# Feed-forward of a two-layer transformer block: the down-projection between the gate half and the value half

## The chip, the cores and the metric

The kernel runs on 1 core of one Trainium2 chip. The time is device time in microseconds, the median of the runs shown. A NeuronCore's engines are named here as in the profile: PE (TensorE, matmuls; PEld is its weight load), DVE (VectorE), ACT (ScalarE), POOL (GpSimd), SP (SyncE, which issues nearly all DMA). They run their own queues in order and wait for one another by semaphores.

## The reference

The inputs are x and ctx of shape 4 x 1024 x 512 in float32. First a banded attention (each query sees the keys within 128 rows), then two layers of local attention and feed-forward. What the change touches is the feed-forward of `_layer`, with HID = 1365:

```python
h = shift_token(x)
mu = h.mean(-1, keepdims=True)
var = h.var(-1, keepdims=True)
h = (h - mu) / jnp.sqrt(var + 1e-05) * lg + lb
h = h @ w1 + b1                       # w1: 512 x 2730
a, g = jnp.split(h, 2, axis=-1)       # value, gate
h = a * jax.nn.gelu(g, approximate=False)
x = x + h @ w2 + b2                   # w2: 1365 x 512
```

## The kernel before

The 4096 rows are 32 tiles of 128 rows (`TILES`). The kernel has a band stage and then, for each of two layers, `attend(l)` and `ffn(l)`. A float32 product is made of three matmuls: every operand is split into a high part, rounded to the type `fp32r`, and the low rest, and TensorE adds high x high, low x high and high x low in PSUM (`products`, L728 to L731, and the loop of `up`, L1069 to L1073).

The feed-forward works on groups of 4 tiles (`GROUP`), so 8 groups (`GROUPS`) of 512 rows in each layer. The 1365 hidden columns are 11 blocks (`HC`): ten of 128 and one of 85 (`FULL`, j = 10). For one group g and one block j:

- `up(l, g, j, 0)` is the gate half: 12 matmuls (4 chunks of the 512 input columns, three each) of 512 rows into one PSUM bank. `up(l, g, j, 1)` is the value half, 12 more into another bank. Three banks go round among the halves (`up_bank`, L365), so the gate half of a block waits until `u` of the block two before it is made, and the value half until the gate of the block before it is read (L1068).
- ACT makes the gate, `gate` (L1401): GELU of the first bank plus bias. DVE makes `u` (`make_u`, L1775): value plus bias, times gate. ACT writes the high part of it into `uT` (`split_u`, L1412, its instruction at L1135), DVE the low part (`split_u`, L1784, its instruction at L1462). The ring of `uT` has three slots.
- `down(g, j)` (L1080) waits for the low part (`uT_low`) and adds the block's share of the output into four banks, one for each tile of the group: 4 x 3 matmuls. For j = 10 in groups 0 to 6 it is a stacked form with 8 matmuls (L1093 to L1099): two transfers on SP (`stack_u`, L681) copy the low part into the unused partitions of `uT`, and `down` waits for them (`u_stacked`), as does ACT's gate of block 1 of the next group (L1407).
- The first `down` of a group overwrites the four banks, so it waits for `f_out` tile by tile: DVE's `finish_group` (L1793, its instruction at L1799) adds the banks of the group before to the residual. It stands in DVE's queue behind `make_u` and `split_u` of block 1 (L1804 to L1811).

In the same period DVE, POOL and ACT prepare the next group's input: `moments`, POOL's `inverse_deviation`, `normalise` at blocks 1, 3, 5, 7; TensorE's transposes `turn_normalised` (L1047) at blocks 3, 5, 7, 9, with the copy on ACT and the low part on DVE (`split_normalised`). In group 0 of each layer the weights of the blocks are split as well: ACT rounds block j+2 behind its part of `uT` (L1434), DVE subtracts (L1809), and ACT writes the high part of block j+1 ahead of the gate of block j (L1428). In the last group of layer 0 ACT and DVE split the next layer's attention weights (L1438 to L1443, L1817).

The order on TensorE is written out by hand in `ffn` (L1105 to L1124). For one block it is gate half, value half, then the down-projection of the block before. At j = 1 that is `down(g - 1, FULL)`, at j = 2 both `down(g, 0)` and `down(g, 1)`, and in j = 0 there is none. Behind the last block of layer 0 come 24 matmuls of the next layer's projection (`project`, L804, L1123) and then `down(GROUPS - 1, FULL)`; behind the last block of layer 1 comes `down` alone. The first halves of a layer (group 0: block 0 and the gate half of block 1) are issued at the end of `attend`.

Of the kernel before, what the change touches and what calls it, by code (L numbers as in the profile page):

```python
# [51 lines left out]
def hid_rows(j):  # L52
    return min(P, HID - j * P)
# [123 lines left out]
def build(nc, x, ctx, mask, wqkv, q_scale, k_scale, wo, ln_g, ln_b, w1, b1, w2, b2, consts, out):  # L177
# [162 lines left out]
    def turned_u(l, g, j):  # L340
        return ffns[l].uT[(g * HC + j) % 3]

    def w1_part(block, j, half, c):
        n = hid_rows(j)
        at = (half * KC + c) * n
        return block[:, at:at + n]

    def w2_part(block, j):
        n = hid_rows(j)
        return block[0:n, 2 * KC * n:2 * KC * n + DIM]  # L350
# [10 lines left out]
    def stacked(g, j):  # L361

        return j == FULL and g < GROUPS - 1

    def up_bank(m):  # L365

        return bank_pair[:, m, :] if m < 2 else banks[2 + (m + 1) % 3]
# [352 lines left out]
    def tensor_program(e):  # L720
# [7 lines left out]
        def products(bank, lhs, rhs, first, last):  # L728
            e.matmul(bank, lhs[0], rhs[0], start=first, stop=False)  # L729
            e.matmul(bank, lhs[1], rhs[0], start=False, stop=False)  # L730
            return e.matmul(bank, lhs[0], rhs[1], start=False, stop=last)  # L731
# [63 lines left out]
        def turn_first_rows(l):  # L795
            n = l * TILES
            w.wait_ge(S("s_in", n % 2), lap(n, 2, 32))
            if l:
                w.wait_ge(S("fhT_low"), n)
            else:  # L800
                w.wait_ge(S("queryT_low"), TILES)
            transposes(rows_bank(l, 0), attends[l].h_in[n % 2], KC, S("h_turned"))

        def project(l, t, first, last):  # L804
            A, base = attends[l], l * TILES
            n = base + t
            for at in range(first, last):
                part, (c, i) = PARTS[at // 12], divmod(at % 12, 3)
                bank = banks[0] if part == 2 else qk_banks(t)[:, part, :]
                if (c, i) == (0, 0):  # L810
                    w.wait_ge(S("hT_low"), n + 1)
                    w.wait_ge(S("attend_weight_high"), KC * (4 * l + at // 12 + 1))
                    if part == 2:
                        w.wait_ge(S("v_rows"), n)
                        w.wait_ge(S("a_out"), base + max(0, t - 3))
                        if t == 0:
                            w.wait_ge(S("f_out") if l else S("keyT_low"), base - 3 if l else TILES)
                    elif t > 1:
                        w.wait_ge(S("with_sin"), 2 * n - 1 + part)
                    elif t:  # L820
                        w.wait_ge(S("f_out") if l else S("x1") if part else S("total_low"),
                                  base - 2 + part if l else TILES if part else BATCH)
                    elif l:
                        w.wait_ge(S("gate") if part else S("u"), l * GROUPS * HC - 1 + part)
                    else:
                        w.wait_ge(S("score_max"), TILES)
                cols = slice(part * DIM, (part + 1) * DIM)
                ins = e.matmul(bank, A.hT[n % 2][:, i % 2, c * P:(c + 1) * P], (wqkv_l if i == 2 else wqkv_h)[:, c, cols],  # L828
                               start=(c, i) == (0, 0), stop=(c, i) == (KC - 1, 2))
                if (c, i) == (KC - 1, 2) and part:  # L830
                    ins.then_inc(S("v_projected") if part == 2 else S("qk_projected"), 1)
# [215 lines left out]
        def turn_normalised(l, t):  # L1047
            n = l * TILES + t
            w.wait_ge(S("ln_normed"), n + 1)
            w.wait_ge(S("fhT_low"), n)  # L1050
            w.wait_ge(S("oT_low"), (l + 1) * TILES)
            transposes(banks[5], ffns[l].h_norm[n % 2], KC, S("fh_turned"))

        def wait_block(l, j):
            w.wait_ge(S("ffn_weight_high"), (HC + 1) * l + (j + 1 if j < FULL else HC + 1))

        def up(l, g, j, order, first=0, last=KC):

            Fm, base, step = ffns[l], l * TILES, l * GROUPS * HC
            n, half = hid_rows(j), 1 - order  # L1060
            hT, m = Fm.hT[g % 2], 2 * (g * HC + j) + order
            bank = up_bank(m)
            w.wait_ge(S("fhT_low"), base + GROUP * (g + 1))
            wait_block(l, j)
            if 2 <= m <= 4:
                w.wait_ge(S("lprobT"), PAIRS * (base + TILES))
            elif m > 4:
                w.wait_ge(S("u") if (m - 3) % 2 else S("gate"), step + (m - 3) // 2 + 1)  # L1068
            for c in range(first, last):  # L1069
                high, low = w1_part(Fm.block_h[j], j, half, c), w1_part(Fm.block_l[j], j, half, c)  # L1070
                e.matmul(bank[0:n, :], high, hT[:, 0, c, :], start=c == 0, stop=False)  # L1071
                e.matmul(bank[0:n, :], high, hT[:, 1, c, :], start=False, stop=False)  # L1072
                ins = e.matmul(bank[0:n, :], low, hT[:, 0, c, :], start=False, stop=c == KC - 1)  # L1073
            if last == KC:
                ins.then_inc(S("up_gate") if half else S("up"), 1)

        def ffn(l):
            Fm, base, step = ffns[l], l * TILES, l * GROUPS * HC

            def down(g, j):  # L1080
                n, q = hid_rows(j), step + g * HC + j
                uT = turned_u(l, g, j)
                w.wait_ge(S("uT_low"), q + 1)
                wait_block(l, j)
                for i in range(GROUP):
                    if j == 0:
                        if g:
                            w.wait_ge(S("f_out"), base + (g - 1) * GROUP + i + 1)
                        else:
                            w.wait_ge(S("a_out"), base + TILES)  # L1090
                            w.wait_ge(S("lprobT"), PAIRS * (base + TILES))
                    rows_of = slice(i * P, (i + 1) * P)
                    if stacked(g, j):  # L1093
                        at = 2 * KC * n
                        w.wait_ge(S("weights_stacked"), 32 * (l + 1))
                        w.wait_ge(S("u_stacked"), 32 * (l * (GROUPS - 1) + g + 1))
                        e.matmul(y_banks[i], uT[:, 0, rows_of], Fm.block_h[j][:, at:at + DIM], start=False, stop=False)
                        ins = e.matmul(y_banks[i], uT[0:2 * SHORT - SPARE, 1, rows_of],
                                       Fm.block_l[j][0:2 * SHORT - SPARE, at:at + DIM], start=False, stop=True)  # L1099
                    else:  # L1100
                        ins = products(y_banks[i], [uT[0:n, h, rows_of] for h in (0, 1)],
                                       (w2_part(Fm.block_h[j], j), w2_part(Fm.block_l[j], j)), j == 0, j == FULL)
                    ins.then_inc(S("down"), 1)

            up(l, 0, 1, 1)  # L1105
            for g in range(GROUPS):
                for j in range(HC):
                    if (g, j) < (0, 2):
                        continue
                    for order in (0, 1):  # L1110
                        up(l, g, j, order)
                    if j == 1:
                        down(g - 1, FULL)
                    if j == 2:
                        down(g, 0)
                    if j >= 2:
                        down(g, j - 1)
                    if g + 1 < GROUPS and j in (3, 5, 7, 9):
                        turn_normalised(l, (g + 1) * GROUP + (j - 3) // 2)
                    if l + 1 < DEPTH and (g, j) == (GROUPS - 1, 9):  # L1120
                        turn_first_rows(l + 1)
            if l + 1 < DEPTH:
                project(l + 1, 0, 12, 36)  # L1123
            down(GROUPS - 1, FULL)  # L1124

        band()
        for l in range(DEPTH):
            attend(l)
            ffn(l)
# [946 lines left out]
```

## Time and profile before

| what | us |
|---|---|
| median of 3 timed runs | 2969.84 (2969.80 to 2969.89) |
| span of the profiled execution (first to last instruction) | 2968.6 |
| PE busy | 2948.6 (99%) |
| DVE busy | 1621.6 (55%) |
| ACT busy | 1228.2 (41%) |
| POOL busy | 1151.9 (39%) |

Of the profiled execution the page gives the span; the time around it is the 1.2 us by which the timed runs exceed it. The busy time of PE is modelled at its ends, so 99% doesn't say that it computes at its peak: matmuls overlap one another. What tells the pace is the distance from one weight load to the next. The feed-forward of layer 0 takes the span from about 854 to 1589 us, that of layer 1 from about 2236 to its end.

### The profile page before, as it was taken

How to read it: one execution, taken by the hardware profiler on the slowest of the kernel's cores; microseconds unless marked ns; L12 is line 12 of the kernel's file. 1: busy time of each engine (PE TensorE's matmuls, PEld its weight loads, DVE VectorE, ACT ScalarE, POOL GpSimd, SP SyncE). 2: the span in 40 equal slices, each digit the busy share in tenths (PEclk: the TensorE clock that was granted, in tenths of full speed). 3: DMA queues.
4: the chain of work that ended last, by engine and by line, in shares of the span. 5: the costliest groups of instructions: out<-in, count | busy, mean ns of one | idle time of the engine just before them, and what ended most of it. 6: DMA issues, size and time to landing. Idle time of an engine off the chain costs nothing. (4 is left out here: it accounts for less than half of the span.)

```text
span 2968.6 us, 44295 instructions
## 1 busy us (share of the span) xinstructions
PE 2948.6 (99%) x17064; PEld 2417.8 (81%) x17064; DVE 1621.6 (55%) x3367; ACT 1228.2 (41%) x2501; POOL 1151.9 (39%) x1190
## 2 busy tenths in 40 slices
PE   9999999999999999999999999999999999999999
PEld 7887888888878888888887888888878888888887
DVE  8976767766664333333425767776775333333331
ACT  7875555555563111111124555555565211111111
POOL 7856666665621110111113556656651111221111
PEclk9999999999999999999999999999999999999999
DMA  6751111111151011100121111111133111111110
GB/s 220 235 186 45 34 51 54 44 44 54 33 158 39 20 40 45 46 31 21 40 96 60 44 43 44 58 47 33 54 93 100 58 45 46 40 59 56 48 49 25
DMA packets 143189, 188.43 MB, mean 63 GB/s; under 512 B 21366, under 2 KB 75130, under 8 KB 142980
## 3 DMA queue, kind: packets, MB, share of 16 engines
q1 hardware_dynamic: 142836, 185.54, 19.5%
q8 instruction: 135, 2.21, 0.3%
q14 instruction: 74, 0.61, 0.1%
q10 hardware_dynamic: 144, 0.07, 0.0%
HBM read 130.34 MB, written 52.46 MB: 62 GB/s over the span
## 5 line engine op out<-in xcount | busy, mean ns | idle before, releaser
L1071 PE MATMUL quad<-fhT_f,w_h_f 128*128 128x512 f32 (+1 forms) x1392 | 550.8, 396 | 0.0
L1073 PE MATMUL quad<-fhT_f,w_l_f 128*128 128x512 f32 (+1 forms) x1392 | 544.9, 391 | 0.0
L1072 PE MATMUL quad<-fhT_f,w_h_f 128*128 128x512 f32 (+1 forms) x1392 | 543.4, 390 | 0.0
L1780 DVE SCALAR_TENSOR_TENSOR u_f<-quad,bias_f,gate_f_raw 128x512 f32<-128x512 f32 (+1 forms) x174 | 130.4, 749 | 705.2 <-PE quad L1073 621.9
L1853 POOL TENSOR_SCALAR stats<-stats 128x1 f32<-128x1 f32 x64 | 43.4, 678 | 1017.1 <-DVE stats L1755 1016.4
L1303 ACT ACTIVATE lprob<-lprob,small 128x384 f32<-128x384 f32 (+2 forms) x512 | 288.6, 565 | 159.4 <-DVE small L1623 159.4
L1947 POOL TENSOR_TENSOR turned_qk<-with_cos,with_sin 128x256 f32<-128x256 f32 x252 | 181.0, 739 | 442.5 <-DVE with_sin L1647 386.4
L1409 ACT ACTIVATE gate_f_raw<-quad,bias_f 128x512 f32<-128x512 f32 (+1 forms) x174 | 119.5, 687 | 512.0 <-PE quad L1073 512.0
L1135 ACT ACTIVATE uT_f<-u_f 128x512 fp32r<-128x512 f32 (+2 forms) x176 | 117.3, 666 | 503.7 <-DVE u_f L1780 503.7
L828 PE MATMUL bank_pair<-wqkv_h,hT 128*128 128x512 f32 x992 | 318.9, 402 | 0.0
L1073 PEld LDWEIGHTS quad<-fhT_f,w_l_f 128*128 128x128 f32 (+1 forms) x1392 | 256.8, 184 | 63.1
L1072 PEld LDWEIGHTS quad<-fhT_f,w_h_f 128*128 128x128 f32 (+1 forms) x1392 | 257.1, 185 | 59.0
L1071 PEld LDWEIGHTS quad<-fhT_f,w_h_f 128*128 128x128 f32 (+1 forms) x1392 | 257.1, 185 | 58.2 <-issue 0.3
L1623 DVE CUSTOM_DVE_ANT_0 lprob<-quad,far 128x384 f32<-128x384 f32 (+2 forms) x512 | 228.7, 502 | 74.4 <-PE quad L920 74.4
L1938 POOL TENSOR_SCALAR lprob<-lprob,small 128x384 f32<-128x384 f32 (+2 forms) x192 | 226.4, 1186 | 26.4 <-DVE small L1608 26.4
L1135 ACT ACTIVATE lprobT<-quad 128x768 f32<-128x768 f32 (+2 forms) x256 | 173.0, 728 | 71.9 <-PE quad L942 69.3
L828 PEld LDWEIGHTS bank_pair<-wqkv_h,hT 128*128 128x128 f32 x992 | 177.4, 189 | 29.8
L828 PE MATMUL bank_pair<-wqkv_l,hT 128*128 128x512 f32 x496 | 200.9, 405 | 0.0
L1888 POOL TENSOR_TENSOR norm<-norm,half_power 128x16 f32<-128x16 f32 x64 | 196.1, 3063 | 5.3
L1462 DVE TENSOR_TENSOR uT_f<-u_f,uT_f 128x512 fp32r<-128x512 f32 x162 | 114.9, 709 | 111.8 <-ACT uT_f L1135 111.8
L959 PE MATMUL bank<-lprobT,v_rows 128*64 128x128 f32 x2688 | 175.0, 277 | 0.0
L959 PEld LDWEIGHTS bank<-lprobT,v_rows 128*64 128x64 f32 x2688 | 144.1, 137 | 34.4 <-issue 31.5
(236 smaller groups left out, 6047.9 us busy)
## 6 DMA issues: line engine op xcount, KB each, us to landing
s_in<-stream SPq DMA_DIRECT2D x128, 128.0 KB, 2.7
s_res<-stream SPq DMA_DIRECT2D x64, 256.0 KB, 2.9
stream<-a_out SPq DMA_DIRECT2D x64, 256.0 KB, 2.0
w_h_f_raw<-in_L_ffn_w SPq DMA_DIRECT2D x60, 256.0 KB, 5.2
h_in_f<-stream SPq DMA_DIRECT2D x112, 128.0 KB, 2.5
res_f<-stream SPq DMA_DIRECT2D x47, 256.0 KB, 3.1
x_in<-in_x SPq DMA_DIRECT2D x32, 256.0 KB, 3.0
x_dram<-x_out SPq DMA_DIRECT2D x32, 256.0 KB, 2.4
```

The costliest lines, as they stand in the source:

```text
L828: ins = e.matmul(bank, A.hT[n % 2][:, i % 2, c * P:(c + 1) * P], (wqkv_l if i == 2 else wqkv_h)[:, c, cols], start=(c, i) == (0, 0), stop= ...
L959: ins = e.matmul(banks[5][half, p * P:(p + 1) * P], A.v_rows[:, k - tiles + 1 + j, h * HD:(h + 1) * HD], A.probT[p % 2][:, i, j * P:(j + 1 ...
L1071: e.matmul(bank[0:n, :], high, hT[:, 0, c, :], start=c == 0, stop=False)
L1072: e.matmul(bank[0:n, :], high, hT[:, 1, c, :], start=False, stop=False)
L1073: ins = e.matmul(bank[0:n, :], low, hT[:, 0, c, :], start=False, stop=c == KC - 1)
L1135: return e.activation(to, source, ACT.Copy)
L1303: e.activation(prob, prob, ACT.Exp, bias=sm[:, h:h + 1], scale=-1.0, accum_out=sm[:, 8 + h:9 + h]).then_inc(S("lprob"), 1)
L1623: e.tensor_tensor_reduce(A.prob[h // 2][:, h % 2, 0:cols], quad[:, pair_banks(h // 2) + h % 2, 0:cols], A.far[:, WIN - cols:], 1.0, BIG, A ...
L1780: e.scalar_tensor_tensor(out=Fm.u[q % 2][0:n, :], in0=up_bank(2 * (g * HC + j) + 1)[0:n, :], scalar=Fm.bias1[0:n, 0, j:j + 1], in1=Fm.gate ...
L1888: e.tensor_tensor(nm[:, 16:32], nm[:, 0:16], half_power[:, :], ALU.pow).then_inc(S("norm_inverse"), 1)
L1938: e.tensor_scalar(prob, prob, sm[:, 16 + 2 * p:17 + 2 * p], None, ALU.mult).then_inc(S("pscaled_pool"), 1)
L1947: e.tensor_tensor(turned[:, :, a:a + h2], cos[:, :, a:a + h2], sin[:, :, b:b + h2], ALU.add).then_inc(S("rotated"), 1)
```

## The change

The down-projections move from behind the value half of a block to a place between its gate half and its value half. The transposes of the next group's input and everything behind them stay behind the value half. Nothing else is edited; the other engines' programs are the same.

```diff
@@ -1107,14 +1107,14 @@
                 for j in range(HC):
                     if (g, j) < (0, 2):
                         continue
-                    for order in (0, 1):
-                        up(l, g, j, order)
+                    up(l, g, j, 0)
                     if j == 1:
                         down(g - 1, FULL)
                     if j == 2:
                         down(g, 0)
                     if j >= 2:
                         down(g, j - 1)
+                    up(l, g, j, 1)
                     if g + 1 < GROUPS and j in (3, 5, 7, 9):
                         turn_normalised(l, (g + 1) * GROUP + (j - 3) // 2)
                     if l + 1 < DEPTH and (g, j) == (GROUPS - 1, 9):
```

## Rows read from the trace of the kernel before

**Rows 1.** The page, part 1: busy us, share of the span, instructions of each engine.
```profile
PE 2948.6 (99%) x17064; PEld 2417.8 (81%) x17064; DVE 1621.6 (55%) x3367; ACT 1228.2 (41%) x2501; POOL 1151.9 (39%) x1190
```

**Rows 2.** Waits of PE and PEld: who waited for whom, us in total, times, longest.
```profile
PE bank_pair L1071 <- DVE fhT_f L1462: 0.8, 2, 0.4
...
PEld quad L920 <- issue: 24.5, 128, 0.6
```

**Rows 3.** Timeline, group 2 of layer 0: start us, us, engine, line, operation, out<-in, [idle before].
```profile
1106.51 0.19 PEld L1071 LDWEIGHTS quad<-fhT_f,w_h_f 128*128 128x128 f32 x1
...
1111.95 0.19 PEld L729 LDWEIGHTS bank<-w_h_f,uT_f 128*128 128x128 f32 x1
...
1112.43 0.75 DVE L1780 SCALAR_TENSOR_TENSOR u_f<-quad,bias_f,gate_f_raw 128x512 f32<-128x512 f32 x1 [6.02 <-PE quad L1073]
...
1113.21 0.63 ACT L1135 ACTIVATE uT_f<-u_f 128x512 fp32r<-128x512 f32 x1 [2.87 <-DVE u_f L1780]
...
1113.88 0.69 DVE L1462 TENSOR_TENSOR uT_f<-u_f,uT_f 128x512 fp32r<-128x512 f32 x1 [0.70 <-ACT uT_f L1135]
...
1114.67 0.59 PEld L725 LDWEIGHTS bank<-ident,h_norm_f 128*128 128x128 f32 x4
...
1115.22 0.15 PEld L1071 LDWEIGHTS quad<-fhT_f,w_h_f 128*85 128x85 f32 x1
```

**Rows 4.** Timeline, end of attention in layer 0: PE waits for DVE.
```profile
833.90 0.67 DVE L1462 TENSOR_TENSOR fhT_f<-bank_pair,fhT_f 128x512 fp32r<-128x512 f32 x1
...
834.62 0.19 PEld L1071 LDWEIGHTS bank_pair<-fhT_f,w_h_f 128*128 128x128 f32 x1 [0.70 <-DVE fhT_f L1462]
...
834.73 0.19 PEld L1072 LDWEIGHTS bank_pair<-fhT_f,w_h_f 128*128 128x128 f32 x1
```

**Rows 5.** Timeline, start of group 3, blocks 1 and 2, layer 0.
```profile
1134.44 0.19 PEld L1097 LDWEIGHTS bank<-w_h_f,uT_f 128*128 128x128 f32 x1
...
1136.31 0.19 PEld L1071 LDWEIGHTS quad<-fhT_f,w_h_f 128*128 128x128 f32 x1
...
1136.97 0.68 DVE L1799 TENSOR_TENSOR res_first_f<-bank,res_first_f 128x512 f32<-128x512 f32 x1
...
1141.82 0.19 PEld L729 LDWEIGHTS bank<-w_h_f,uT_f 128*128 128x128 f32 x1
```

**Rows 6.** Timeline of DVE, group 0 of layer 0: `u` of blocks 3 and 4.
```profile
878.53 0.75 DVE L1780 SCALAR_TENSOR_TENSOR u_f<-quad,bias_f,gate_f_raw 128x512 f32<-128x512 f32 x1 [6.40 <-PE quad L1073]
...
887.75 0.73 DVE L1780 SCALAR_TENSOR_TENSOR u_f<-quad,bias_f,gate_f_raw 128x512 f32<-128x512 f32 x1
```

**Rows 7.** Timeline, last block of layer 0.
```profile
1578.06 0.19 PEld L729 LDWEIGHTS bank<-w_h_f,uT_f 128*128 128x128 f32 x1
...
1579.86 1.90 ACT L1135 ACTIVATE wqkv_h<-wqkv_h_raw 128x2048 fp32r<-128x2048 f32 x1
```

**Rows 8.** Timeline, last block of layer 1.
```profile
2959.31 0.19 PEld L729 LDWEIGHTS bank<-w_h_f,uT_f 128*128 128x128 f32 x1
...
2961.24 0.69 DVE L1462 TENSOR_TENSOR uT_f<-u_f,uT_f 85x512 fp32r<-85x512 f32 x1 [0.70 <-ACT uT_f L1135]
```

**Rows 9.** Timeline after block 10, group 2; DMA issues: count, KB each, us to landing.
```profile
1120.63 0.19 PEld L729 LDWEIGHTS bank<-w_h_f,uT_f 128*128 128x128 f32 x1
...
1123.70 1.48 SPq L421 DMA_DIRECT2D uT_f<-gate_f  x2
...
w_h_f_raw<-in_L_ffn_w SPq DMA_DIRECT2D x60, 256.0 KB, 5.2
...
stream<-a_out SPq DMA_DIRECT2D x64, 256.0 KB, 2.0
```

**Rows 10.** Busy us in stretches (x instructions), then granted clock, DMA share, GB/s.
```profile
0.00:10.00 10.00, 6.78 (x30) 5.34 (x30) 3.77 (x8) 5.10 (x9) 5.64 (x18) 1.00 0.82 275
...
858.90:931.00 72.10, 72.10 (x324) 59.44 (x323) 41.10 (x48) 34.54 (x39) 8.99 (x11) 1.00 0.34 93
...
2895.00:2959.00 64.00, 64.00 (x279) 51.33 (x278) 10.36 (x14) 9.93 (x15) 8.46 (x7) 1.00 0.04 13
```

## The prediction

> **What bounds the kernel now.** I read the page first: TensorE is busy for 99% of the span, VectorE for 55% [rows 1]. Then the waits of TensorE: they belong to the band and attention stages. The feed-forward's own lines appear with 0.8 us in 2 waits, before its first group [rows 2], and its down lines never for a wait on `uT`. So TensorE has no gap in the feed-forward and sets its time. An order of the same instructions can't take anything from a queue without gaps; it can only open gaps. The question is how much earlier each `down` now asks for its `uT`, and whether the chain that makes `uT` is ready.
>
> In the timeline I take as T the moment when TensorE begins its first weight load after a value half. For one block T is 1111.95 [rows 3]. The down-projection of 12 matmuls behind it takes 1114.67 - 1111.95 = 2.72 us, the two halves ahead of it 1111.95 - 1106.51 = 5.44, so one half 2.72; the four transposes take 1115.22 - 1114.67 = 0.55 [rows 3]. In the odd groups the two halves from 1136.31 to 1141.82 give 2.75 each [rows 5]. The chain to `uT` is VectorE `u` at T+0.48, ScalarE's high part at T+1.26, VectorE's low part from T+1.93 to T+2.62 [rows 3].
>
> When TensorE really waits for VectorE, its load begins 0.05 us after the end of VectorE's instruction (833.90 + 0.67, then 834.62), and its second load follows after 0.11 instead of 0.23 us [rows 4]. So a load that begins up to 0.12 us late costs nothing, since in a full stream it stands that far ahead of its matmul.
>
> **The change, part by part.** No instruction is added or removed. The sum is made against the span of the profiled execution, 2968.6 us; the median of the timed runs, 2969.84, lies 1.2 us above it, and I carry that over.
>
> (a) Plain blocks. Before, between a value half and the down-projection that needs its `uT` stood a down-projection and two halves, 8.2 us. Now only the next gate half stands there. It is over at T+2.72, the load may come at T+2.84 for nothing, and `uT` is there at T+2.62+0.05 = T+2.67. Margin 0.17 us, 0.20 in odd groups. Such blocks are j = 2, 4, 6, 8 in groups 0 to 6 and j = 2 to 9 in group 7: 36 per layer, 72 in all; where j is odd in groups 0 to 6, transposes add 0.55. Value: 0. Bounds: nothing, or, if the wait costs what an "issue" gap costs in attention (24.5 us in 128, that is 0.19 [rows 2]), 0.19 x 66 = 12.5 us (6 of the 72 are in (c)). I take 0, since the directly awaited load [rows 4] is the same kind of wait.
>
> (b) Group borders. `down(g, 0)` waits for `f_out`, VectorE's additions of the preceding group. These stand in VectorE's queue behind `u` and `uT` of block 1. Before, block 1's value half was followed by `down(g-1, FULL)`, and then two halves: 7.4 us cover. Now `down(g-1, FULL)` stands ahead of the value half, and only gate half 2 is left. With T = 1134.44 the first addition begins at 1136.97 and lasts 0.68 [rows 5]: end T+3.21, load T+3.26. Wanted at T+2.75+0.12 = 2.87 (odd groups) or 2.84 (even): a gap of 0.39 or 0.42. The other three additions last 0.68 at most and a quarter of `down` takes 0.68, so they cost nothing. Odd groups 4 and even ones 3 per layer: 2 x (4 x 0.39 + 3 x 0.42) = 5.6 us. Bounds: 0, if the additions got ahead, and 0.68 more each time (14 x 0.68 = 9.5) if one addition more counted. VectorE is free for block 2 in time, as value half 2 now ends 11 us after T.
>
> (c) Group 0, where the weights are split too. From `u` of an odd block to the `u` of the next takes 887.75 - 878.53 = 9.22 us, an unbroken chain: copy of weights on ScalarE, their low part and the normalisation on VectorE, the low part of `fhT` [rows 6]. The next `u` is wanted after 0.55 + 3 x 2.72 = 8.71 us. So it is 0.5 late, `uT` at T+3.17 against T+2.84: 0.33 us at j = 4, 6, 8, twice: 2.0 us. Before, the same lateness was covered by the down-projection. The rest of the work of the weights (finish of block j+1 before the gate of j) stays ahead of TensorE: block 3 moves by 2.6 us for TensorE, and by about as much for the other engines. Bounds 0 and 0.5 x 6 = 3.0.
>
> (d) End of layer 0. After value half 10 follows the projection of the next layer, whose second part needs the high part of the last weights. ScalarE makes it behind its part of `uT`: 1579.86 + 1.90 = T+3.70 with T = 1578.06 [rows 7]. Before, the last but one down-projection stood between (2.75 us); the second part was wanted at T+5.5. Now at T+2.72, or 2.84: gap 3.75 - 2.84 = 0.9 us. The following chain hangs on the end of `down(7, FULL)` and moves as a whole. Bounds 0 and 1.0.
>
> (e) End of layer 1. `down(7, FULL)` now follows its own value half at once. `uT` is there at 2961.24 + 0.69 - 2959.31 + 0.05 = T+2.67 [rows 8], wanted at T+0.12: 2.55 us. The instructions behind it are unchanged. Bounds 2.3 and 2.7.
>
> (f) The stacked block. Its two transfers are issued from T+3.07 to T+4.55 (1123.70 + 1.48, T = 1120.63) [rows 9], and are wanted by `down(g-1, FULL)` at T+8.2, before at T+10.9. The trace gives no landing time for them. The nearest row is 2.0 us for stores of that queue, the farthest 5.2 for the weights' loads [rows 9]. 4.55 + 2.0 = 6.55, so nothing; with 5.2, 1.5 us x 14 = 21 us would be possible. I take 2.0, a transfer out of SBUF too. ScalarE's gate of block 1 also waits for it, but only from T+8.2. The Trainium skill ("SBUF — State Buffer", section on the DMA setup-cost knee) says that every transfer pays a roughly fixed 2 us whatever its size. By that they land by T+6.6, and the sum stays as it is; the 2.0 us rows agree.
>
> The reload of weights on SyncE waits for `down` counts that now come a half earlier: nothing is late. Sum: 0 + 5.6 + 2.0 + 0.9 + 2.55 + 0 = 11.05 us. Span 2979.65, time 2980.9.
>
> There is a rule that speaks against the change: the Trainium skill ("TensorE: Matmul & The Clock Gate", Part 1) has the clock throttled by default and released only by activity. The gaps added here are at most 2.55 us. In the stretch 0 to 10 us TensorE is busy for 6.78 of 10 us, at the granted clock 1.00 [rows 10], so I see no sign of it. As a mechanism of this kernel: if the clock fell to its lower level (1.2 GHz) after gap (e), the last 12 matmuls would take 2.75 us longer, 2983.7.
>
> **Rivals.**
> 1. The plain blocks do stall: the margin of (a) is only 0.17 us, made of a 0.05 and a 0.12 that I have from the attention's side. 66 gaps of 0.1 to 0.19 us give 6.6 to 12.5 more, 2987.5 to 2993.4. For it: the many "issue" gaps of 0.19 [rows 2]; against it: two awaited loads at 0.05.
> 2. It hides: the additions of (b) and the lateness of (c) fall inside what TensorE has queued; only (d) and (e) remain, 2973.3. Against it: VectorE's order is fixed in the code.
> 3. Faster. Halves take 2.75 in odd groups and 2.72 in even ones [rows 3, 5], where 512 columns at 2.4 GHz are 0.213, 12 of them 2.56 us. If that excess of 0.16 to 0.19 came from ScalarE and VectorE reading PSUM while TensorE writes it, the other order could shift it. There are some 528 such stretches (16 groups x 33); from 0.021 us less in each it would pay for the 11 us, and with 0.03 less it gives 2980.9 - 16 = 2965. Against it: the stretch 858.9 to 931, in which VectorE is busy for 41.10 of 72.10 us, has the quick halves, and 2895 to 2959 with 10.36 of 64 the slow ones [rows 10].
> 4. The stacked transfers come late, 1.5 us in each of 14 borders: 3002. Nothing speaks for it but the missing row.
> 5. The clock falls: 2983.7, above.
>
> **How the numbers follow.** Changes under 0.2% (5.9 us) can hardly be told from none. Chances: forecast 0.66 (its own range 2978 to 2985), rival 1 0.15, rival 2 0.11, rival 3 0.04, rival 4 0.03, rival 5 0.01. Slower by over 0.2% (over 2975.8): 0.66 + 0.15 + 0.03 + 0.01, less 0.02 for a forecast that ends small: 0.83. Within 0.2%: 0.11 + 0.02 = 0.13. Faster 0.04. The range goes from 2974, near rival 2, to 2994, the end of rival 1.
>
> **What would show it.** In the profile after: TensorE waiting for VectorE's additions (`res`, some 0.4 us, 14 times), for `uT` in group 0 (0.3 us, 3 times a layer) and once for 2.5 us at the end, for `wqkv_h` once for 0.9. `u` at T+0.48 and the low part ending at T+2.62, as before, and loads of `down` in plain blocks at T+2.72 without idle time. I would be wrong if waits for `uT` stand there 60 times and more, if the transfers of `gate` into `uT` release `down(g-1, FULL)`, or if a half itself takes another time than 2.72 or 2.75.

## The result, and the profile after

| kernel | median us | runs | span of the profiled execution | its own time |
|---|---|---|---|---|
| before | 2969.86 | 2969.80 to 2970.73 | 2968.6 | |
| after | 3010.48 | 3008.45 to 3011.70 (4) | 3006.6 | 3008.45 |

The ratio of the runs is 1.0135 (95% interval 1.0121 to 1.0150): slower by 1.35%, 40.6 us. I had forecast slower by 11 us, range 2974 to 2994. The sign was right; the size and the range were wrong. The profiled execution after is the fastest of its four, 38.6 us above the median before; the other three took 1.4 to 3.3 us more.

The page after, against [rows 1]: span, then busy time by engine. The instruction counts are unchanged; the span grew by 38.0 us.

```profile
span 3006.6 us, 44295 instructions
PE 2960.7 (98%) x17064; PEld 2415.7 (80%) x17064; DVE 1621.1 (54%) x3367; ACT 1221.2 (41%) x2501; POOL 1150.6 (38%) x1190
```

The waits after, first of TensorE's matmuls (the line, what it waited for: us in total, times, longest), against [rows 2], where no down-projection waited for anything:

```profile
PE bank L1097 <- DMA uT_f<-gate_f: 18.9, 14, 1.5
PE bank L729 <- DVE uT_f L1462: 4.1, 6, 2.3
PE bank L729 <- DVE res_first_f L1799: 3.5, 14, 0.3
PE quad L828 <- ACT wqkv_h L1135: 0.6, 1, 0.6
```

Then of the weight loads, which stand in front of the matmuls and show the full gap:

```profile
PEld bank L1097 <- issue: 24.5, 14, 1.9
PEld bank L729 <- DVE uT_f L1462: 13.2, 18, 2.7
PEld bank L729 <- issue: 5.8, 11, 0.6
PEld quad L828 <- ACT wqkv_h L1135: 1.0, 1, 1.0
```

L1097 is the first instruction of the stacked `down(g - 1, FULL)`. It waits 14 times, once for each group border that has one (7 per layer), and the releaser is the transfer of the low part into `uT`. That is the row that my prediction named as one that would prove it wrong. The other three lines are the waits I had expected, at about the price I had given them.

I measured the loss from weight load to weight load, phase by phase, in both traces:

| step of the prediction | forecast us | measured us |
|---|---|---|
| (f) gate half 1 and stacked down, 14 borders | 0 | +22.2 |
| (b) gate half 2, until the additions | 5.6 | +6.5 |
| (c) group 0 | 2.0 | +2.4 |
| (d) end of layer 0 | 0.9 | +0.97 |
| (e) end of layer 1 | 2.55 | +2.67 |
| (a) plain blocks: base | 0 | 0 |
| (a) plain blocks: 5 stretched low parts | not seen | +2.4 |
| remaining pace of halves | 0 | +1.3 |
| sum, against a span longer by 38.0 | 11.05 | 38.4 |

**One border.** The timeline after, at the border from group 2 to group 3 of layer 0 (start, duration, engine, line, operation; in brackets the idle time and what ended it), against [rows 5, 9]. T is 1128.77.

```profile
1129.25 0.75 DVE L1780 SCALAR_TENSOR_TENSOR u_f<-quad,bias_f,gate_f_raw 85x512 f32<-85x512 f32 x1 [6.00 <-issue]
1131.12 0.69 DVE L1462 TENSOR_TENSOR gate_f<-u_f,uT_f 85x512 fp32r<-85x512 f32 x1 [1.13 <-ACT uT_f L1135]
1131.83 1.48 SPq L421 DMA_DIRECT2D uT_f<-gate_f  x2
1136.80 0.19 PEld L1073 LDWEIGHTS quad<-fhT_f,w_l_f 128*128 128x128 f32 x1
1138.75 0.69 ACT L1409 ACTIVATE gate_f_raw<-quad,bias_f 128x512 f32<-128x512 f32 x1 [2.58 <-DMA uT_f<-gate_f]
1138.77 0.19 PEld L1097 LDWEIGHTS bank<-w_h_f,uT_f 128*128 128x128 f32 x1 [1.79 <-issue]
```

Up to the issue everything stands where I had put it: `u` at T+0.48, transfers issued from T+3.06 to T+4.54. TensorE's last load of gate half 1 is at 1136.80, and the next one should come 0.23 later at T+8.26. It comes at 1138.77, T+10.0, and ScalarE's gate of block 1, which waits for the same transfers, starts at the same moment (1138.75). So the transfers landed 5.4 us after the issue of the second ended, not 2.0. The load of L1097 is 1.74 us late. One block later in the same border, `down(g, 0)` behind the additions:

```profile
1145.23 0.69 DVE L1462 TENSOR_TENSOR uT_f<-u_f,uT_f 128x512 fp32r<-128x512 f32 x1 [0.70 <-ACT uT_f L1135]
1145.84 0.68 DVE L1799 TENSOR_TENSOR res_first_f<-bank,res_first_f 128x512 f32<-128x512 f32 x1
1145.82 0.19 PEld L1073 LDWEIGHTS quad<-fhT_f,w_l_f 128*128 128x128 f32 x1
1146.64 0.19 PEld L729 LDWEIGHTS bank<-w_h_f,uT_f 128*128 128x128 f32 x1 [0.64 <-issue]
```

The addition ends at 1146.52 and the load follows 0.12 later. It is put down to "issue", since the last releaser in the profile (`uT`) had long come. Of its distance of 0.82 to the load before, 0.23 is the usual one: 0.59 idle more, of which 0.12 costs nothing. That is the 0.46 (6.5 in 14) of the table.

**What the trace of before could have told.** The activity of the DMA engines in the same border, before (T = 1120.63, issue at 1123.70 [rows 9]): 40 slices of 0.2 us, busy tenths and GB/s; then the GB/s of the stretch 1130 to 1131 alone, in slices of 0.025 us.

```profile
DMA  0000000000100044263576744531000000000000
GB/s 0 0 0 0 0 0 0 0 0 10 20 0 10 20 92 82 92 41 67 169 179 220 246 138 138 184 128 67 31 20 31 20 31 20 31 20 26 20 26 0
GB/s 0 0 82 0 0 41 0 41 41 0 41 0 41 41 0 41 0 41 0 41 41 0 41 0 41 0 41 41 0 41 0 41 0 0 0 0 0 0 0 0
```

The stretch of the first two lines is 1123 to 1131. Packets flow until the last slice but one, 1130.8, which is T+10.2. From 1128.6 on it is a thin tail of 20 to 31 GB/s. Nothing but the two stacked transfers (rows of 2 KB) and two loads of `h_in_f` issued behind them (rows of 1 KB) was under way. A slice of 0.025 us with 82 GB/s is the start of one row of 2 KB, one with 41 that of a row of 1 KB. So the last row of the stacked transfers went at 1130.05 and was over at T+9.5; what follows belongs to the loads. In the trace after, the last row of 2 KB ends at T+9.5 too, and the release comes 0.5 us behind it. So a landing at T+9.5 at the earliest, or at T+10.2 if the end of all packets is taken for it, was there to be read. The need of before was ScalarE's gate of block 1 at T+10.9 (it ran at 1132.11) and `down` at 1134.44, T+13.8. My prediction gave 10.9 for the need of `down`, which is the gate's, and said that the trace gives no landing time. The tail of after, seen closer, in 1137 to 1138 (GB/s in slices of 0.025 us):

```profile
GB/s 82 0 0 82 0 0 0 82 0 0 82 0 0 82 0 0 82 0 0 82 0 0 0 82 0 0 82 0 0 82 0 0 82 0 0 82 0 0 0 82
DMA packets 14, 0.03 MB, mean 27 GB/s; under 512 B 1, under 2 KB 1, under 8 KB 14
q1 hardware_dynamic: 14, 0.03, 6.9%
```

Of the 14 packets 13 are rows of 2 KB (the fourteenth is the one under 512 B), one every 0.08 us, and the share of 6.9% of 16 engines is 1.1 engines. So about one engine is moving rows one after another, and the others move next to nothing; 43 rows at 0.08 us are 3.4 us. The experiments below show whose rows they are.

### The profile page after: what moved, and what is told of

Read it like the earlier page. It is cut to its first block and busy times, and to the rows that moved or that the text cites. A ratio compares the mean times of both kernels' runs of the same rounds, so it can differ in the third digit from the quotient of the medians.

```text
span 3006.6 us, 44295 instructions
## 1 busy us (share of the span) xinstructions
PE 2960.7 (98%) x17064; PEld 2415.7 (80%) x17064; DVE 1621.1 (54%) x3367; ACT 1221.2 (41%) x2501; POOL 1150.6 (38%) x1190
```

## The experiments

All diffs are against the kernel after unless said otherwise. "New order" is gate half, down-projection, value half; "old order" is that of before. The kernels of one group share their runs of the kernel before, whose median was 2970.26, 2970.56 and 2970.09 in the three groups below.

### First group: which of the causes carry what

**stack32** cuts the transfer of 43 rows in two, 32 and 11, with the counts of the semaphore raised from 32 to 48 per border in both waits. It leaves the order alone.

```diff
-load(uT[SHORT:P, 0, :].bitcast(F32), low_u[0:SPARE, :].bitcast(F32), S("u_stacked"))
+load(uT[SHORT:SHORT + 32, 0, :].bitcast(F32), low_u[0:32, :].bitcast(F32), S("u_stacked"))
+load(uT[SHORT + 32:P, 0, :].bitcast(F32), low_u[32:SPARE, :].bitcast(F32), S("u_stacked"))
```

> The changed order, with the first transfer of the stacked block (43 rows of 2 KB) cut into 32 and 11 rows; the second, of 42 rows, is left. In the changed kernel TensorE stands 1.55 us net at each of 14 group borders, because these transfers land some 9.9 us after the value half. Theory A: the 43 rows go one after another through one DMA engine, 0.14 us each, 6 us together; cut, all three transfers land about T+7.5 and the gaps go: 14 x 1.55 = 21.7 us less than the changed kernel, 2989. Theory B: the time is the fixed cost of a transfer between two SBUF places and the loads of h_in issued right behind it take the engines; then the cut adds an issue (0.7 us) and the gap stays or grows: 3010 to 3020.

Measured 2989.27 (2987.43 to 2989.89), ratio 1.0063 (1.0048 to 1.0078): 21.2 us of the 40.6 are back. The waits at L1097 are gone. The gate of block 1 at the first border is now released by TensorE itself, and the DMA engines carry the data wide and early (948 to 949, slices of 0.025 us):

```profile
949.54 0.69 ACT L1410 ACTIVATE gate_f_raw<-quad,bias_f 128x512 f32<-128x512 f32 x1 [1.28 <-PE quad L1074]
GB/s 287 205 410 246 205 246 246 328 164 492 246 328 369 287 410 123 369 287 328 328 164 83 123 82 41 41 0 41 41 0 0 0 0 0 0 0 0 0 0 0
```

So the loss at the borders hangs on the shape of a transfer, and not on its bytes (one issue more, the same 170 KB in all). I had expected 0.14 us for a row on the one engine; it is 0.08.

**finish_first** moves VectorE's additions of the old group ahead of `u` and `uT` of block 1.

```diff
+                    if g and j == 1:
+                        finish_group(g - 1)
                     if (g, j) > (0, 0):
                         make_u(l, g, j)
                     split_u(l, g, j)
...
-                    if g and j == 1:
-                        finish_group(g - 1)
```

> The changed order, with VectorE's additions of the preceding group put ahead of u and uT of block 1. Theory A: TensorE's gap ahead of down(g, 0), 0.47 us net at 14 borders, comes from VectorE's order: 6.6 us less than the changed kernel, 3004. Theory B: the gap is the down-projection's own, started after a long wait; the time stays at 3010 within 1 us.

Measured 3003.00 (3001.94 to 3004.23), ratio 1.0111 (1.0095 to 1.0126): 7.5 us less. The wait for `res_first_f` is gone, and the stacked one stays as it was, so (b) and (f) are apart:

```profile
PEld bank L1097 <- issue: 24.4, 14, 1.9
```

**pool_small** lets GpSimd add the bias and the residual in one column of 512 only (its output lacks them elsewhere).

```diff
-e.tensor_tensor(res, res, Fm.bias2[:, :], ALU.add)
+e.tensor_tensor(res[:, 0:1], res[:, 0:1], Fm.bias2[:, 0:1], ALU.add)
...
-e.tensor_tensor(res, res, (Fm.x1_last if is_last(l, t) else Fm.x1_in)[:, :], ALU.add)
+e.tensor_tensor(res[:, 0:1], res[:, 0:1], (Fm.x1_last if is_last(l, t) else Fm.x1_in)[:, 0:1], ALU.add)
```

> The changed order; GpSimd's additions of bias 2 and of x1 to the residual are done on one column instead of 512 (the output lacks them elsewhere). Theory A: in plain blocks the margin is under 0.2 us and holds, except where GpSimd's addition runs beside VectorE's low part of uT and stretches it from 0.69 to up to 1.78 us; and the lateness of group 0 comes from the same stretch of the normalisation (1.71 instead of 0.75 us). Then the long low parts and the gaps of group 0 are gone: 2.6 + 2 = 4 to 5 us less than the changed kernel, 3006, and its runs no longer spread over 3 us. Theory B: the long low parts have another cause (transfers into SBUF): they stay, at most 2 us less.

Measured 3006.37 (3005.62 to 3007.08), ratio 1.0122 (1.0107 to 1.0137): 4.1 us less, and the runs lie 1.5 us apart instead of 3.3. The waits of the loads for `uT` fall from 13.2 us in 18 to

```profile
PEld bank L729 <- DVE uT_f L1462: 7.7, 8, 2.7
```

All six waits of group 0 are gone, which are the 2.4 us of (c), and four of the five behind stretched low parts, 1.6 of their 2.4 us. Together 4.0.

**border_back** has the old order at j = 1 alone, so `down(g - 1, FULL)` stands behind the value half again.

```diff
+                    value_first = j == 1
+                    if value_first:
+                        up(l, g, j, 1)
                     if j == 1:
                         down(g - 1, FULL)
...
-                    up(l, g, j, 1)
+                    if not value_first:
+                        up(l, g, j, 1)
```

> The changed order, but at j = 1 the value half stands ahead of down(g-1, FULL) again. Theory A: the border's two gaps (stacked transfers 21.7 us, additions 6.6 us) both hang on this one place: 28 us less than the changed kernel, 2982. Theory B (my forecast's rival 1: the plain blocks stall too): only part of the 40 us hangs on the borders, less than 20 us are gained.

Measured 2980.91 (2980.30 to 2982.69), ratio 1.0036 (1.0024 to 1.0049): 29.6 us less. This one line of the order is worth (f) and (b) together (22.2 + 6.5 = 28.7), since `down(g, 0)` gets its cover back too.

### Second group: how wide the margins are

**from_block3** is the form of border_back with `value_first = j < 3`: the new order in blocks 3 to 10 only.

> The changed order from block 3 on only; blocks 0, 1 and 2 keep the old one. No border gap is left, all 72 plain down-projections are still started right after a gate half. Theory A (plain blocks have a margin of 0.17 to 0.20 us): what is left of the 40 us is group 0 (2.0), the ends of the layers (3.7), a few stretched low parts (2 to 4) and some 2 us of other pace: 2980 to 2982, as with the old order at j = 1 alone. Theory B (the plain blocks lose 0.1 to 0.2 each): 2984 or more.

Measured 2981.84 (2981.01 to 2984.17), ratio 1.0039 (1.0024 to 1.0054). Old order at j = 2 brings nothing beyond border_back, in agreement with theory A.

**down_earlier** and **down_later** take that kernel as their base and move the down-projection by one chunk of 3 matmuls (0.68 us): ahead of the last chunk of the gate half, or behind the first chunk of the value half. (`up` takes a range of chunks.)

```diff
+                    value_first = j < 3
+                    gate_part, value_part = (KC, KC) if value_first else (3, 0)   # down_later: (4, 1)
+                    up(l, g, j, 0, 0, gate_part)
+                    if value_part:
+                        up(l, g, j, 1, 0, value_part)
...
+                    if gate_part < KC:
+                        up(l, g, j, 0, gate_part, KC)
+                    if value_part < KC:
+                        up(l, g, j, 1, value_part, KC)
```

> As the changed order from block 3 on, but the down-projection stands ahead of the last quarter of the gate half, 0.68 us (3 matmuls) earlier. This measures the margin. Theory A (0.17 to 0.20 us in plain blocks, uT ready at T+2.67): each of 66 plain ones opens a gap of 0.68 - 0.18 = 0.50, the 6 late ones of group 0 0.68 more, the 56 behind transposes almost none (0.03): 33 + 4 + 2 = 39 us over the same kernel without it, 3020. Theory B (margin zero or below, each already stalls): 0.68 x 72 = 49 over it. Theory C (a margin of half a us and more): under 15 over it.

Measured 3015.24 (3014.74 to 3016.75), ratio 1.0152 (1.0135 to 1.0169), 33.4 us above from_block3; I had expected 39. The waits of the loads for `uT`, and a plain block in which `uT` ends at 1098.03:

```profile
PEld bank L729 <- DVE uT_f L1469: 59.9, 113, 2.9
1097.34 0.69 DVE L1469 TENSOR_TENSOR uT_f<-u_f,uT_f 128x512 fp32r<-128x512 f32 x1 [0.70 <-ACT uT_f L1142]
1098.09 0.19 PEld L729 LDWEIGHTS bank<-w_h_f,uT_f 128*128 128x128 f32 x1 [0.68 <-DVE uT_f L1469]
```

Here TensorE asks at 1097.45 (1097.22 + 0.23) and gets its load 0.64 later, of which 0.12 is free: 0.52 us per plain block. The trace has 45 such waits (idle 0.63 to 0.68) and 4 longer ones; 57 more loads, behind transposes, stand idle for 0.20 to 0.26. I had counted 66 plain places. In this order there are 49, since `down(g, 2)` has the two down-projections of block 2 as cover and waits nowhere; 17 places at 0.5 are 8.5 us of my 39. With 0.68 less cover 0.52 are lost, so the margin in the plain blocks was 0.68 - 0.52 = 0.16; (a) had said 0.17.

> As the changed order from block 3 on, but the down-projection stands behind the first quarter of the value half, 0.68 us later. Theory A: the lateness of 0.33 in group 0 goes (2.0 us), and gaps of up to 1.05 us from stretched low parts shrink to 0.37 (1 to 2 us); the ends of the layers stay: 3 to 4 us less than the same kernel without it, 2977. Theory B: cutting a half in two costs pace at 128 places, 0.03 us and more each: no gain or some us more.

Measured 2976.61 (2975.37 to 2977.62), ratio 1.0020 (1.0011 to 1.0030), 5.2 us below from_block3. What is left of the waits for `uT` is the end of layer 1 and little else:

```profile
PEld bank L729 <- DVE uT_f L1469: 4.1, 5, 2.7
```

**stack42** is stack32 with the cut at 42 and 1.

> The changed order, with the first transfer of the stacked block (43 rows) cut into 42 rows and 1. Theory A: 43 is prime, so its rows can't be shared out evenly and go through one engine; 42 can (as in the second transfer, which is left): all of the 21.7 us are gained, as with 32 and 11 rows, 2989. Theory B: the number of rows on an engine is what counts and 42 is served like 43: nothing is gained, 3010.

Measured 2988.57 (2987.29 to 2989.80), ratio 1.0060 (1.0045 to 1.0075): as good as 32 + 11. Taking a single row out of 43 is enough; it isn't the size of the pieces. Theory A was right, theory B is out.

### Third group: ends, the mended kernel, and the border alone

**ends_back** has the old order in group 0 and in the very last block: `value_first = (g == GROUPS - 1 and j == HC - 1) or g == 0`.

> The changed order, but group 0 of each layer and the last block of each layer keep the old order. Theory A: the gaps of group 0 (0.33 us at three blocks, 2.0 us in both layers), of the end of layer 0 (0.97) and of the end of layer 1 (2.7) go, nothing else: 5.6 us less than the changed kernel, 3004.5 to 3005. Theory B: what is saved at the end of layer 0 is lost again in the attention behind it, whose chain starts later: 4.7 us or less.

Measured 3000.41 (2999.19 to 3002.33), ratio 1.0102 (1.0088 to 1.0116): 10.1 us less, where I had expected 5.5 to 6. I had missed that the old block 10 of group 0 also gives the first border of each layer its cover back: 12 waits instead of 14, which is 2 x 1.6 = 3.2 of the difference. With the 5.6 that makes 8.8; the other 1.3 may be the clock, which no longer falls at the end (rival 5 below), and the scatter of the runs.

```profile
PEld bank L1097 <- issue: 21.1, 12, 1.9
```

**mended** joins stack32, finish_first and ends_back.

> The changed order with all mends together: the 43 rows cut into 32 and 11, VectorE's additions ahead of block 1's u, the old order in group 0 and in the last blocks. Theory A: of the 40 us there stay the stretched low parts of uT (some 3 gaps of 0.4 to 1.05 us) and about 2 us of other pace: 2974 to 2976, slower than before by 0.15 to 0.2%. Theory B: the effects hid one another and at least another 5 us appear: over 2979. Faster than the kernel before (under 2970.2) would say that the order has a gain of its own, for which nothing in the traces speaks.

Measured 2975.78 (2973.61 to 2976.74, 11 runs), ratio 1.0018 (1.0009 to 1.0026). The new order with its three causes taken away is still 5.7 us slower than before. In the profiled execution, whose span is 4.1 us longer than that of before, 5 waits for `uT` stand idle for 4.7 us, 3.9 net of what is free, all behind stretched low parts:

```profile
PEld bank L730 <- DVE uT_f L1467: 4.7, 5, 1.1
```

**only_border** is the reverse: old order everywhere but at j = 1 (`value_first = j != 1`), so that `down(g - 1, FULL)` alone stands between halves.

> The old order everywhere but at j = 1, where down(g-1, FULL) stands between the halves. Theory A: the stacked transfers land some 9.9 us after the value half of block 10, and here 10.9 us of cover (down(9), three halves) are left, so no gap from them; the additions (done 3.3 us after the value half of block 1) have two halves of cover: 2970 to 2971. Theory B: the place itself costs something (a pace, ScalarE's later gate): 2975 and more.

Measured 2970.18 (2969.84 to 2970.45, 10 runs), ratio 1.000 (0.999 to 1.0009). Here `down(9)` stands behind the value half of block 10, so `down(g - 1, FULL)` is wanted at T+10.9 and the transfers, landing at T+10.0, are in time. The same move costs 29 us where the cover of the transfers, and that of the additions, is 2.7 us shorter, and nothing here.

No version beats the kernel before. It has no gap in the feed-forward that an order could close, and one version (only_border) equals it.

## Why the prediction was wrong, step by step

**(f) is the step that failed.** It is a term mis-sized, 0 against 22.2 us. The place and the wait stood there, and rival 4 even had a price, 1.5 us in each of 14 borders, close to the 22.2 / 14 = 1.59 measured. That is luck: its 5.2 us are the landing of the weights' loads, other transfers with another cause. What was wrong is the choice of 2.0 us landing, by the nearest rows, and the chance of 0.03 that came from it; measured are 5.4 us from the end of the issue. Those rows are stores of whole tiles of 128 rows. The transfer in question has 43 rows, and a store of another shape is no measure for it. The DMA activity of before, shown above, would have given an estimate, a landing between T+9.5 and T+10.2 against a need of T+8.26. Less the 0.12 that is free, the gap is 1.1 to 1.8 us, 16 to 25 us in 14 borders, and the total 2997 to 3006.

Beside that choice I had put the Trainium skill, "SBUF — State Buffer", section on the DMA setup-cost knee, a fixed 2 us. The measurement differs: 6.9 us from the first issue to the release. Another page of the Trainium skill speaks to the case and I had not used it: "DMA: Bandwidth & Descriptors", section on why a DMA increments its semaphore by 16 and not by 1. It says that such a copy is split over as many engines, at most 16, as divide the outermost size of both sides. By that rule 43 rows go to one engine, 42 to 14, 32 to 16 and 11 to 11. The 6.9% share of the tail and both cuts agree with it. What no run here shows is the rule for other sizes.

**(b) held.** 6.5 against 5.6. A gap is 0.46 and not 0.39 to 0.42, since a load that waits for the additions begins 0.12 us after their end here (1146.52, then 1146.64), and not 0.05 as in [rows 4]. finish_first, whose one edit concerns these waits, gave 7.5 by the medians and 6.8 by the same steps of its trace.

**(c), (d), (e) held.** 2.4, 0.97 and 2.67 against 2.0, 0.9 and 2.55. In group 0 the prediction's terms put `u` of block 4 at 878.53 + 2.61 + 9.22 = 890.36 (2.61 is what block 3 moved by) and the load at 892.55. The trace after has them at 890.36 and 892.54:

```profile
888.12 1.71 DVE L1766 SCALAR_TENSOR_TENSOR h_norm_f<-h_norm_f,stats,shift_f 128x512 f32<-128x512 f32 x1 [0.80 <-POOL stats L1854]
890.36 0.74 DVE L1780 SCALAR_TENSOR_TENSOR u_f<-quad,bias_f,gate_f_raw 128x512 f32<-128x512 f32 x1
892.54 0.19 PEld L729 LDWEIGHTS bank<-w_h_f,uT_f 128*128 128x128 f32 x1 [0.58 <-DVE uT_f L1462]
```

What makes that chain 9.22 us long I had not asked. The normalisation, L1766, takes 1.71 us beside GpSimd's addition of the bias; in pool_small, where that addition is one column, it takes 0.75, and the six waits are gone (first line after, second pool_small):

```profile
887.99 1.30 POOL L2000 TENSOR_TENSOR res_first_f<-res_first_f,bias_f 128x512 f32<-128x512 f32 x1
888.25 0.75 DVE L1766 SCALAR_TENSOR_TENSOR h_norm_f<-h_norm_f,stats,shift_f 128x512 f32<-128x512 f32 x1 [0.80 <-POOL stats L1854]
```

The end of layer 1, against [rows 8]: the load stands idle for 2.75 us, 0.08 of it more than I had counted.

```profile
2999.51 0.69 DVE L1462 TENSOR_TENSOR uT_f<-u_f,uT_f 85x512 fp32r<-85x512 f32 x1 [0.69 <-ACT uT_f L1135]
3000.26 0.19 PEld L729 LDWEIGHTS bank<-w_h_f,uT_f 85*128 85x128 f32 x1 [2.75 <-DVE uT_f L1462]
```

The end of layer 0, against [rows 7]:

```profile
1599.19 1.90 ACT L1135 ACTIVATE wqkv_h<-wqkv_h_raw 128x2048 fp32r<-128x2048 f32 x1
1601.14 0.30 PEld L828 LDWEIGHTS quad<-wqkv_h,hT 128*128 128x128 f32 x2 [1.04 <-ACT wqkv_h L1135]
```

**(a) held where nothing disturbs the chain, and has a hole where something does.** Gate halves ahead of a plain down-projection take 2.72 and 2.75 us, as before, and down_earlier shows the margin, 0.16. Rival 1 is out. But a margin of 0.16 us can't absorb a longer instruction in the chain. GpSimd's addition (L2005) beside VectorE's low part:

```profile
2418.76 0.63 ACT L1135 ACTIVATE uT_f<-u_f 128x512 fp32r<-128x512 f32 x1 [5.69 <-DVE u_f L1780]
2419.36 1.29 POOL L2005 TENSOR_TENSOR res_f<-res_f,x_in_f 128x512 f32<-128x512 f32 x1 [1.46 <-DMA x_in_f<-x_dram]
2419.43 1.78 DVE L1462 TENSOR_TENSOR uT_f<-u_f,uT_f 128x512 fp32r<-128x512 f32 x1 [0.70 <-ACT uT_f L1135]
2421.26 0.19 PEld L729 LDWEIGHTS bank<-w_h_f,uT_f 128*128 128x128 f32 x1 [1.05 <-DVE uT_f L1462]
```

The low part takes 1.78 instead of 0.69 us, ends 0.56 after GpSimd's 2420.65, and the load stands idle for 1.05. The trace of before has four such low parts (0.95 to 1.75 us long, as at 2579.26), and 8.2 us of cover hid them; after there are five, 2.4 us in all, each beside a GpSimd addition of bias or input to the residual (L2000, L2005). They fall in other blocks from trace to trace; GpSimd's addition in the lines above had waited for a transfer. pool_small, which all but removes these additions, keeps one of the five, beside another GpSimd instruction (L1881), and its runs are steadier.

**Rivals 2 and 3.** Rival 2 (hidden) fails with the waits for `res_first_f`. Rival 3 (quicker halves) fails too: the halves got slower by 1.3 us in all, mostly value halves. Why that is stays open.

**Rival 5 is not out.** In the trace after, the clock stays at 1.00 (2.4 GHz) through the last down-projection, behind the wait of (e). The same wait of 2.75 us stands in nine of the traces kept. In three (after, from_block3, stack42) the clock held through that down-projection; in six (stack32, finish_first, pool_small, border_back, down_earlier, down_later) it fell to 0.50, its lower level of 1.2 GHz, at most 2.0 us after the wait ended. In the last 50 us before the wait TensorE had no gap over 0.1 us (0.7 in down_earlier); then it stood idle for the 2.75. The last down-projection in after and in pool_small (the stretch; busy us of PE, PEld, DVE, ACT, POOL; granted clock; DMA):

```profile
3000.20:3003.10 2.90, 2.84 (x12) 2.18 (x12) 1.77 (x4) 0.00 (x0) 0.00 (x0) 1.00 0.07 27
2996.50:3001.30 4.80, 4.80 (x11) 3.77 (x12) 1.90 (x3) 0.00 (x0) 0.00 (x0) 0.50 0.19 73
```

From the first load of that down-projection to the end of the span it is 6.38 or 6.39 us where the clock held, and 7.19 to 8.81 where it fell: 0.8 to 2.4 us more, against the 2.75 that the prediction had put on it. So rival 5's mechanism is real, its cost is small beside (f), and a chance of 0.01 was low for it. It may be a part of what the other three executions of after took longer than the profiled one; no trace of them is kept. ends_back and mended, which don't have the wait, don't have the fall. A gap of 2.86 us inside the feed-forward (down_earlier, at 1567.7) and the 14 of up to 1.89 us at the borders left the clock at 1.00.

## What to carry to other kernels

When a change takes cover from a wait, list every transfer that the cover was hiding, and read when its bytes end in the DMA activity of the trace before; a landing time taken from a transfer of another shape isn't an answer, and where it is unknown, both ends belong in the range with real chances. A piece of work with no gap on the engine that bounds it can only lose by a new order, so the forecast is made of the smallest margins left, and a margin of 0.2 us isn't one if another engine can lengthen an instruction in the chain. An average clock of 0.999 can hide a fall in the last 9 us: read the clock of the stretch behind each long gap. Give a transfer that is waited for a row count that divides well.

## What the runs showed of the hardware

- A copy inside SBUF of 43 rows of 2 KB, issued together with one of 42 rows, landed 6.9 us after its issue, with one packet of 2 KB every 0.08 us near its end. Cut into 32 + 11 or 42 + 1 rows, it was no longer awaited by T+8.3, 1.7 us sooner at least, at the price of one issue more, 0.8 us on SyncE.
- VectorE's addition with both inputs in SBUF (0.69 us) and the normalisation at L1766 ended 0.54 to 0.56 us after a GpSimd addition that had started just before them. The Trainium skill ("SBUF — State Buffer", section on who interferes with whom) has such a VectorE instruction contend with one of GpSimd that reads SBUF, one blocking the other for its whole length. The trace agrees: 1.78 us is what was left of GpSimd's 1.29, and 0.56.
- Behind a gap of 2.75 us ahead of the last down-projection the granted clock fell from 1.00 to 0.50 (2.4 to 1.2 GHz) in six of nine traces, and the end of the kernel took 0.8 to 2.4 us more there. Gaps of up to 2.86 us inside the feed-forward left it at 1.00.
